# Scan stage of a hybrid kernel: C rows spread by DMA, one scan over both halves, products in place on two engines, D term and residual on TensorE

## What is computed

```
xc, z  = split(x @ in_w.T);  xc = silu(conv(xc) + conv_b)
dt, Bm, Cm = split(xc @ xp_w.T)            # 8, 16 and 16 columns
delta  = softplus(dt @ dtp_w.T + dtp_b);  A = -exp(A_log)
# for each token t and each state entry n:
h = exp(delta_t * A) * h + (delta_t * u_t) * B_t
y_t = sum over n of h * C_t
y = (y + xc * D) * silu(z);  out = y @ out_w.T
```

## Time and profile before

| | us |
|---|---|
| median of 3 runs | 6968.48 (6958.11 to 6979.99) |
| profiled execution, its own time | 6968.54 |
| its span in the profile | 6966.8 |
| scan stage, first to last scan | 141.6 to 2039.8 |

### The profile page before, as it was taken

The page is one execution under the profiler, slowest core; times in us unless marked ns, Lnnn a source line. Parts: engine busy times, 40 slices in busy tenths (PEclk is TensorE's granted clock), DMA queues, the critical chain, the costliest instruction groups (busy, mean ns, idle before and its releaser), DMA issues. The chain is left out here.

```text
span 6966.8 us, 82050 instructions
## 1 busy us (share of the span) xinstructions
PE 5471.0 (79%) x22698; PEld 2779.7 (40%) x22762; DVE 4363.1 (63%) x6931; ACT 2835.7 (41%) x4713; POOL 3229.9 (46%) x2381
## 2 busy tenths in 40 slices
PE   4888888888878877798996888853996778784697
PEld 1333333333324344342782444422663333333465
DVE  5999999999985620575224666742675455552575
ACT  4655666666644532354222333421332233341232
POOL 3888888888863400252212333316333344434433
PEclk8999999999999855897557999966997899995898
DMA  1133111111100000000002222212452333211355
GB/s 65 73 134 134 73 73 73 73 73 72 68 36 0 0 0 0 0 0 4 0 0 73 73 69 61 55 74 69 164 190 93 78 72 69 74 27 54 119 188 176
DMA packets 174787, 476.12 MB, mean 68 GB/s; under 512 B 29648, under 2 KB 54992, under 8 KB 146640
## 3 DMA queue, kind: packets, MB, share of 16 engines
q1 hardware_dynamic: 156272, 434.28, 19.5%
q0 software_dynamic: 18176, 37.79, 1.6%
HBM read 364.87 MB, written 107.07 MB: 68 GB/s over the span
## 5 line engine op out<-in xcount | busy, mean ns | idle before, releaser
L337 POOL TENSOR_TENSOR mamba_bu<-mamba_du,mamba_b_all 128x1024 f32<-128x1024 f32 x512 | 1200.5, 2356 | 280.5 <-DVE mamba_hc L599 268.9
L592 DVE TENSOR_TENSOR_SCAN mamba_bu<-psum,mamba_bu 128x512 f32<-128x512 f32 x1024 | 1193.2, 1206 | 157.3 <-ACT psum L529 124.7
L428 PE MATMUL psum<-mamba_hc,consts 128*128 128x512 f32 x2048 | 1017.8, 621 | 31.7 <-DVE mamba_du L604 28.6
L529 ACT ACTIVATE psum<-mamba_delta,A 128x510 f32<-128x510 f32 x1024 | 684.6, 685 | 570.2 <-DVE mamba_bu L592 556.2
L599 DVE TENSOR_TENSOR mamba_hc<-mamba_bu,psum 128x1024 f32<-128x1024 f32 x512 | 611.7, 1195 | 6.1 <-PE psum L419 3.9
L428 PEld LDWEIGHTS psum<-mamba_hc,consts 128*128 128x128 f32 x2048 | 403.6, 198 | 370.3 <-issue 350.9
L1598 POOL DMA_INDIRECT results<-ffn_moe_y_rows,ffn_moe_row_of x312 | 302.1, 968 | 506.4 <-DVE ffn_moe_y_rows L1788 430.8
L2355 POOL TENSOR_TENSOR loc_q_bd<-loc_q_max,weights_l1a 128x512 fp32r<-128x512 f32 x256 | 260.6, 1049 | 585.2 <-DVE loc_q_max L2587 565.5
L1713 ACT ACTIVATE ffn_moe_act<-ffn_moe_act 128x512 f32<-128x512 f32 x344 | 216.9, 630 | 683.4 <-DVE ffn_moe_act L1757 435.6
L2355 POOL TENSOR_TENSOR cau_q_bd<-cau_q_max,weights_l1b 128x512 fp32r<-128x512 f32 x256 | 258.1, 1040 | 448.9 <-DVE cau_q_max L2587 434.1
L2578 DVE TENSOR_REDUCE cau_top<-psum 128x2 f32<-128x512 f32 (+1 forms) x384 | 264.1, 692 | 291.5 <-PE psum L2422 278.6
(11 more groups left out here) (395 smaller groups left out, 11786.3 us busy)
## 6 DMA issues: line engine op xcount, KB each, us to landing
mamba_b_all<-b_rows SPq DMA_DIRECT2D x128, 1024.0 KB
ffn_moe_w_gu<-gate_up_parts SPq DMA_DIRECT2D x78, 1024.0 KB
pairs<-empty_rows SPq DMA_DIRECT2D x6, 3432.0 KB, 15.3
ffn_moe_got<-pairs SPq DMA_DIRECT2D x78, 264.0 KB, 3.3
ffn_moe_w_down<-in_l_moe SPq DMA_DIRECT2D x78, 256.0 KB
qk_rows<-loc_qk SPq DMA_DIRECT2D x16, 1024.0 KB, 10.7
ffn_moe_back<-results SPq DMA_DIRECT2D x32, 512.0 KB, 4.6
qk_rows<-cau_qk SPq DMA_DIRECT2D x16, 1024.0 KB, 4.3
```

The lines of the kernel that those rows point to most:

```text
L337: nc.gpsimd.tensor_tensor(bu[:, J % BU, :, :], du[:, q % 2, :, :], b, ALU.mult).then_inc(bu_ready, 1)
L428: nc.tensor.matmul(ysum[h], mem.ident, hc[:, J % HC, h, :], start=(n == 0), stop=(n == NST - 1), skip_group_check=True).then_inc(summed, 1)
L529: nc.scalar.activation(by_seq(dA[i % DECAYS])[:, :, 1:S], by_seq(delta[:, q % 2, h, :])[:, :, 1:S], ACT.Exp, scale=mem.A[:, q % 2, h * NST ...
L592: nc.vector.tensor_tensor_scan(bu[:, J % BU, h, :], dA[i % DECAYS], bu[:, J % BU, h, :], 0.0, ALU.mult, ALU.add).then_inc(scanned, 1)
```

## The change

- C rows: the matmul `spread_c` and the splitting into bf16 parts are gone. The 16 B rows and 16 C rows are written to HBM together, and each load brings two B rows and two C rows (1 MB) into `bc_all`, four slots in a ring, eight loads a unit. A slot is loaded again once the products that read it are done.
- Scan: one instruction over both halves, 128x1024. dA is now two buffers of two banks.
- Product with C: in place in bu, with both operands in SBUF. Steps 4, 9 and 14 of each unit are POOL's (behind its drive three steps later), the other 13 are DVE's. bu has 8 buffers in place of 4; hc is gone.
- `reduce` runs four steps behind in PE's order. At n = 0 it first adds the D term, by a matmul of u with a diagonal matrix `skip`, made once by DVE from the identity and D.
- `gated` on DVE now multiplies ysum in PSUM with silu(z), both halves in one instruction, at n = 4. POOL's `gate` is gone.
- `out` on PE adds X by a third matmul with the identity; ACT's eviction writes X itself. POOL's residual sum is gone.

The diff of `mamba`, cut to its core:

```diff
-    CHUNK = 4
-    BU, HC, DECAYS = 4, 3, 3
+    CHUNK, SLOTS = 2, 4
+    CHUNKS = NST // CHUNK
+    BU = 8
+    LATE = 3
...
+        bc_all = sb("bc_all", [SLOTS, 2, CHUNK, T])
         bu = sb("bu", [BU, 2, T])
-        hc = sb("hc", [HC, 2, T])
-        dA = [mem.bank[i] for i in range(DECAYS)]
-        c_bc = mem.bank[3]
+        dA = mem.psum[:, 0:4, :].rearrange("p (a h) t -> p a h t", a=2)
...
+        def by_pool(J):
+            return J % NST in (4, 9, 14)
...
+                    if chunk >= SLOTS:
+                        wait_weighed(sp, CHUNK * (chunk - SLOTS + 1) - 1)
+                    rows = b_rows[q % 2].rearrange("(a n) t -> a (n t)", a=2)[:, c * CHUNK * T:(c + 1) * CHUNK * T]
+                    sp.dma_start(bc_all[:, chunk % SLOTS, :, :, :].rearrange("p a n t -> p a (n t)"),
+                                 rows.unsqueeze(0).to_broadcast([D, 2, CHUNK * T])).then_inc(bc_landed[chunk % SLOTS], 16)
...
             def drive(q, n):
-                pool.wait_ge(hc_ready, J - BU + 1 + LEAD)
+                pool.wait_ge(summed, J - BU + 1 + LEAD)
...
+            def weigh(J):
+                pool.wait_ge(scanned, J + 1 + LEAD)
+                nc.gpsimd.tensor_tensor(bu[:, J % BU, :, :], bu[:, J % BU, :, :], c, ALU.mult).then_inc(weighed_pool, 1)
...
                     drive(q, n)
-                    if n == 5 and q >= 1:
-                        gate(q - 1)
-                    if n == 10 and q >= 1:
-                        out(q - 1)
-                    if n == 11 and more:
-                        split_rest(q + 1)
-                    if n == 13 and more:
-                        split_last(q + 1)
+                    if J >= LATE and by_pool(J - LATE):
+                        weigh(J - LATE)
...
             def reduce(J):
+                if n == 0:
+                    pe.wait_ge(y_ready, q + LEAD)
+                    for h in range(HALVES):
+                        nc.tensor.matmul(ysum[:, h, :], mem.skip[:, d, h, :], u[:, d, h, :], start=True, stop=False, skip_group_check=True)
...
             def out(q):
+                nc.tensor.matmul(by_seq(to), mem.ident, in_time(by_seq(X[:, tokens(q)]), q), start=False, stop=True, skip_group_check=True).then_inc(work_ready, 1)
...
             def scan(J):
-                for h in range(HALVES):
-                    i = 2 * J + h
-                    dve.wait_ge(dA_ready, i + 1 + LEAD)
-                    nc.vector.tensor_tensor_scan(bu[:, J % BU, h, :], dA[i % DECAYS], bu[:, J % BU, h, :], 0.0,
-                                                 ALU.mult, ALU.add).then_inc(scanned, 1)
+                dve.wait_ge(dA_ready, 2 * J + 2 + LEAD)
+                nc.vector.tensor_tensor_scan(in_row, dA[:, J % 2, :, :].rearrange("p h t -> p (h t)"), in_row, 0.0,
+                                             ALU.mult, ALU.add).then_inc(scanned, 1)
             def weigh(J):
-                nc.vector.tensor_tensor(hc[:, J % HC, :, :], bu[:, J % BU, :, :], c_bc.unsqueeze(1).to_broadcast([D, 2, T]), ALU.mult).then_inc(hc_ready, 1)
+                nc.vector.tensor_tensor(bu[:, J % BU, :, :], bu[:, J % BU, :, :], c, ALU.mult).then_inc(weighed_vector, 1)
             def gated(q):
+                nc.vector.tensor_tensor(du[:, q % 2, :, :], ysum, z[:, q % 2, :, :], ALU.mult).then_inc(y_ready, 1)
```

More of the change, by code:

```diff
@@ L266, in tokens, with wait_weighed, place @@
             return slice(q // 2 * T, q // 2 * T + T)
+        def by_pool(J):
+            return J % NST in (4, 9, 14)
+        pool_until, vector_until = [0], [0]
+        for J in range(NST * UNITS):
+            pool_until.append(pool_until[-1] + by_pool(J))
+            vector_until.append(vector_until[-1] + (not by_pool(J)))
+        def wait_weighed(eng, J):
+            eng.wait_ge(weighed_vector, vector_until[J + 1] + LEAD)
+            eng.wait_ge(weighed_pool, pool_until[J + 1] + LEAD)
+        def place(J):
+            chunk = J // CHUNK
+            return chunk % SLOTS, J % CHUNK
         @block.sync
@@ L276, in _ @@
                 sp.wait_ge(work_read, position["xdbl", q, 0] + 1 + LEAD)
[L277 to L284, removed]
+                sp.dma_start(b_rows[q % 2], xdbl[32:32 + 2 * NST, :]).then_inc(bc_stored, 16)
+                sp.wait_ge(bc_stored, 16 * (q + 1) + LEAD)
+                for c in range(CHUNKS):
+                    chunk = q * CHUNKS + c
+                    if chunk >= SLOTS:
[3 more added lines that the diff above has]
+                                 rows.unsqueeze(0).to_broadcast([D, 2, CHUNK * T])).then_inc(bc_landed[chunk % SLOTS], 16)
                 if 4 <= q < 4 + 2 * RING:
@@ L403, in project_u @@
                 for h in range(HALVES):
[L404 removed]
+                    last = nc.tensor.matmul(to[0:64, :], w["xp_" + DIRS[d]][:, h * 64:(h + 1) * 64], u[:, d, h, :],
                                             start=(h == 0), stop=(h == 1))
@@ L462, in _ @@
                             project_gate(q + 1, n - 12)
-            reduce(NST * UNITS - 1)
+            for J in range(NST * UNITS - LATE - 1, NST * UNITS):
+                reduce(J)
             out(UNITS - 1)
@@ L611, in _ @@
                     scan(J)
-                    if J >= 1:
+                    if J >= 1 and not by_pool(J - 1):
                         weigh(J - 1)
-                    if n == 1 and q >= 1:
+                    if n == LATE + 1 and q >= 1:
                         gated(q - 1)
@@ L2757, in pack_mamba @@
         out["out_" + c] = g("out_w")
-    for start in (64, 96):
-        out["from_%d" % start] = (np.arange(D)[:, None] >= start).astype(np.float32)
     out["proj"] = rows_in_halves(i["L0_attn_a_proj_w"].T)
@@ L2865, in one_hot_columns @@
             sel[k * NE + e, e] = 1.0
-        for n in range(2 * NST):
-            sel[32 * (k + 1) + n, NE + n] = 1.0
     return sel
```

144 lines of the change are left out of this document (51 added, 93 removed).

## The result

| | before | after |
|---|---|---|
| median of 17 runs each, us | 6966.24 (6935.44 to 6998.05) | 7021.57 (6978.33 to 7045.22) |
| profiled execution: its own time, its span | 6968.54, 6966.8 | 7021.57, 7019.8 |
| first to last scan | 141.6 to 2039.8 | 140.0 to 2116.1 |
| a unit (of 32) | 59.3 | 61.75 |
| behind the scan stage, from the next stage's first cast to the end | 4907.5 | 4886.5 |

The ratio is 1.0074, with 1.0056 to 1.0091 as its interval: the change costs some 52 to 55 us. It is slower, as forecast, and the time lies in the stated range, but the forecast of 7099 was 77 us too high: it had the change cost 131 us, and the 55 measured are less than half of that.

The account below looks back on a forecast made before the run. DVE was taken to bound the kernel before, at 59.3 us a unit; queueing with POOL would make it 63.5. 6968.54 + 32 x (63.5 - 59.3) - 4 gives 7099 us, range 7000 to 7240.

Parts of the forecast that it names:

- DVE's own work: Scan stage, DVE per unit: 16 merged scans at 2.19, 13 products at 1.12, gate 1.2; sum 50.8 us.
- POOL's work: Scan stage, POOL per unit: 21 operations of 1024 at 2.33 plus gaps of 0.55; sum 49.5 us.
- The queue: Scan stage: DVE products with two SBUF operands and POOL operations go in turn, 3.30 us a pair, 62.1 a unit.
- DVE first: Scan stage: DVE gets its turn whenever both engines want it; 62.1 us a unit, 7054 us in all.
- The order at the hand-over: Scan stage: DVE goes ahead of POOL in two of three; 62.1 + 4.2 / 3 = 63.5 us a unit.
- the part behind the stage: Later stages, behind the scan stage: they run the same instructions, so their change was cost at nothing.
- The ends of the stage: Ahead of the first scan and behind the last sum: net 4 us gained, between 0 and 8.
- (1) No contention: Scan stage: the in-place product doesn't queue with POOL; 54.7 us a unit, 6817 us, faster; chance 0.06.
- (2) A shorter hold: Scan stage: long operations wait for part of the other's rest only; 6936 to 7054 us; chance 0.08.
- (3) POOL always first: Scan stage: DVE's product waits until POOL has nothing to issue; a unit near 85 us, 7790 us; chance 0.04.
- (4) Loads late: Scan stage, loads of B and C rows: twice the bytes arrive late; 7190 to 7240 us; chance 0.04.

## Why the prediction held in its mechanism and missed the size

**DVE's own work: right.** A merged scan's pitch is 2.20 (1493.00 to 1495.20), taken as 2.19; product 1.12 (1503.56 to 1504.68) and thirteen a unit. The scans' waits for ACT fell from 124.7 to 75.9; I had said that ACT would release none.

**POOL's work: right.** 21 operations a unit, and the gaps of 0.18 ahead of L323 and 0.37 behind it are the same as in the earlier trace rows.

**The queue: right, and the heart of the case.** The rule read from 512-wide operations of another stage holds for 1024: 2.22 and 1.08 in the rows above against 2.21 and 1.09. The stretch of POOL is 0.90 a product, predicted 3.30 - 2.33 = 0.97. The pair of kernels that differ in one operand shows the cause by itself, 302 us. That POOL takes DVE's place as the bound shows in its 98.3% and in the waits of the scans. With the 62.1 of "DVE first" the stage was sized to 0.35 us a unit.

**The order at the hand-over: the step that failed.** "I take DVE first in two of three, 62.1 + 4.2 / 3 = 63.5" added 1.4 us to a unit, 45 us in all, and it was wrong twice. DVE is first nearly always (3 products of 416 passed over). And being passed over costs the unit next to nothing: with 40 passed over it grew by 0.27 us. Without this term the forecast is 7054, a cost of 86 us. I had added POOL's further operation to the unit, though by my own sum POOL's sequence was already the bound and contains that operation in either order. A wait of an engine with slack had been charged as if it were on the path.

**Sizes.** The rest of the gap of 77 us: 0.35 us a unit below 62.1, 11 us in all, and 21 us in the part behind the stage, which I cost at nothing. 45 + 11 + 21 = 77. The first of the two smaller ones repeats (61.75 and 61.74 a unit in the two executions): the stretch is 0.07 a product less than summed, 0.9 a unit, and POOL's idle time is 32.9 / 32 = 1.0 in place of 0.55. The second is of the size of the spread between runs, and its cause stays open. The ends of the stage gave what was said: the first scan comes 1.6 earlier (141.6 to 140.0) and the way from the last scan's end to the cast is 17.2 in place of 19.5, together 3.9 of the 4.

**The rivals.** (1) No contention: fallen, products at 1448 ns on the mean and POOL's operations at 2.91. (2) A shorter hold: its time, 6936 to 7054, contains the 7021.57 measured, so the time alone doesn't refute it; the rows do, since both directions show a full hold to 0.01. (3) POOL always first: fallen. (4) Loads late: no idle time of POOL is released by a DMA, and all of its idle time ahead of the four groups is 56.6 us, 22.9 of them one wait for ACT ahead of the first L317; a load takes 5.3 us to landing on the page of after. With no product on POOL, 10.6 us of such waits do appear.

**What a better sum would have been.** 62.1 a unit and the 4 us of the ends give 7054, the end that the forecast named for "DVE first". It would still have been 33 too high, by the two smaller terms.

## What to carry to other kernels

Before work is moved to POOL, count which operations of DVE beside it read two tiles in SBUF: in this kernel each such pair took about 3.3 us (1503.56 to 1506.88 above), little less than the 1.19 and 2.35 of the two one after the other, and the sum over POOL's sequence, not either engine's own total, was the bound to compare. Leaving one operand in PSUM, even at the cost of a matmul to bring it there, was worth 302 us between twins and 158 us against the change itself, and with it the same three products on POOL turned from a loss of 70 us into a gain of 76. And where two engines queue, first ask which of them is the bound: the order in which they go changes the time only as far as it makes that one wait.

## What the runs showed that I had not expected

- The hand-over is decided by hundredths of a us, and DVE's product, mostly 0.03 to 0.06 ahead, wins nearly each time; 0.04 later it still wins the ties, and 40 of 416 are passed over instead of 3. I had expected such a margin to be noise.
- A buffer count and the order of two matmuls on PE (C from PSUM, six buffers) cost 7% against the kernel before, nearly ten times what the change itself costs, in a kernel meant to be faster.
- The part of the program behind the stage, with the same instructions, took between 4886.5 and 4919.7 us in two executions each of the two kernels, and shorter in the slower kernel both times.
